# Moving the next group's norm, window sums and patch copies to other places among the sampling tiles of a fused four-layer convolution kernel

## Time and profile before

| | us |
|---|---|
| median of 3 runs | 2766.87 (2762.34 to 2772.3) |
| the profiled execution's own time | 2759.06 |
| its span, first to last instruction | 2757.2 |
| PE, DVE, ACT busy | 2132.4, 1811.6, 1524.7 |
| from one front's second convolution to the next one's | 327.8 |

### The profile page before, as it was taken

One profiled execution on the slowest core, in us unless ns is written; L12 is line 12 of the kernel. 1 busy time (PEld: TensorE's weight loads), 2 busy tenths in 40 slices (PEclk: granted clock), 3 DMA queues, 4 the chain that ended last, 5 costly groups with the idle time before them and its releaser, 6 DMA issues.

```text
span 2757.2 us, 51316 instructions
## 1 busy us (share of the span) xinstructions
PE 2132.4 (77%) x20658; PEld 1792.4 (65%) x20658; DVE 1811.6 (66%) x3534; ACT 1524.7 (55%) x1803; POOL 24.7 (1%) x35
## 2 busy tenths in 40 slices
PE   0274488787886978878788778878788798887999
PEld 0223465687666966578666776568766696667998
DVE  3365458667686666866677665866758665776776
ACT  0021356466564655556565465646656465656987
POOL 1000000000000000000000000000000000000000
PEclk9686699899998989989999889989899899998999
DMA  6643533273351842436333453327434182113331
GB/s 171 126 132 72 141 106 120 76 161 113 100 147 43 202 123 78 125 92 181 103 105 104 111 155 106 116 79 161 119 98 148 44 199 92 52 48 90 108 116 56
DMA packets 290577, 311.50 MB, mean 113 GB/s; under 512 B 238148, under 2 KB 249092, under 8 KB 286116
## 3 DMA queue, kind: packets, MB, share of 16 engines
q1 hardware_dynamic: 285828, 273.74, 36.5%
q0 software_dynamic: 3360, 30.27, 4.1%
q10 hardware_dynamic: 1152, 4.19, 0.5%
HBM read 251.65 MB, written 56.48 MB: 112 GB/s over the span
## 4 chain that ended last, share of the span: by engine, by line
PE 53%; DVE 19%; DVEq 8%; SPq 7%; ACT 5%; DMA 4%; issue 4%; ACTq 0%; POOL 0%; POOLq 0%
PE bank L1014 37%; PE bank L1096 5%; SPq L369 4%; DVE code L884 4%; DVEq L883 4%; PE bank L1001 3%; DVE samp L713 3%; PE bank L1115 2%; SPq L319 2%; DVE strip L708 2%; PE bank L1074 1%; DVEq L712 1%; ACT diag L581 1%; PE bank L1132 1%; PE bank L1156 1%
## 5 line engine op out<-in xcount | busy, mean ns | idle before, releaser
L1014 PE MATMUL bank<-picture,tent 128*128 128x160 f32 x9216 | 1420.5, 313 | 79.1 <-DVE strip L708 52.2
L1014 PEld LDWEIGHTS bank<-picture,tent 128*128 128x128 f32 x9216 | 1351.5, 201 | 109.5 <-issue 83.2
L708 DVE TENSOR_TENSOR strip<-bank,near 128x480 f32<-128x480 f32 x768 | 503.6, 656 | 586.2 <-PE bank L1014 585.3
L514 ACT ACTIVATE tent<-zs,row_at_sb 128x1152 f32<-128x1152 f32 x512 | 614.5, 1249 | 50.5 <-DMA zs<-z_rows 50.3
L517 ACT ACTIVATE tent<-tent 128x2304 f32<-128x2304 f32 x256 | 543.8, 2124 | 18.8 <-issue 1.7
L713 DVE TENSOR_REDUCE samp<-strip 128x96 f32<-128x480 f32 x768 | 501.5, 653 | 72.4 <-issue 2.7
L504 ACT COPY samp_t<-bank 96x384 f32<-96x384 f32 x256 | 120.6, 471 | 461.9 <-PE bank L1001 461.8
L1115 PE MATMUL bank<-cb,xs 128*128 128x512 f32 x512 | 267.3, 624 | 118.6 <-DVE code L884 86.4
L1115 PEld LDWEIGHTS bank<-cb,xs 128*128 128x128 f32 x512 | 83.3, 191 | 259.4 <-issue 173.7
L574 ACT COPY xs<-xn 32x128 f32<-32x128 f32 x256 | 75.0, 293 | 195.6 <-PE bank L1115 177.8
L1001 PE MATMUL bank<-ident_sb,samp 128*96 128x128 f32 x768 | 138.5, 292 | 53.3 <-ACT fin L500 47.4
(11 more groups left out here) (125 smaller groups left out, 1061.5 us busy)
## 6 DMA issues: line engine op xcount, KB each, us to landing
zs<-z_rows SPq DMA_DIRECT2D x256, 576.0 KB, 4.2
picked_weights<-arena SPq DMA_DIRECT2D x15, 1800.0 KB
arena<-picked_weights SPq DMA_DIRECT2D x24, 720.0 KB, 6.6
arena<-windows SPq DMA_DIRECT2D x288, 50.0 KB, 4.0
slice<-picked_weights SPq DMA_DIRECT2D x16, 720.0 KB, 6.1
windows<-arena SPq DMA_DIRECT2D x32, 312.5 KB, 5.0
slice<-windows SPq DMA_DIRECT2D x192, 50.0 KB, 2.9
y_patches<-yc SPq DMA_DIRECT2D x32, 160.0 KB, 4.4
```

Of the source, the lines that this page charges most:

```text
L514: act.activation(w[:, c], zs[:, N % SPREADS, :], ACT.Abs, bias=row_at[:, c:c + 1])
L708: dve.tensor_tensor(y, STRIPS[j % 3][:, 0:DENSE * XW * C].rearrange("p (d c x) -> p d c x", d=DENSE, c=C), w.broadcast_to([128, DENSE, C, ...
L1014: m = pe.matmul(STRIPS[j % 3][:, XW * C * e:XW * C * (e + 1)], tent[:, N % TENTS, c, DENSE * d + e], picture[:, b % 2, i, c], start=(c == ...
```

## The change

DVE's `features(k)` becomes two parts: `normalise(k)` (wait for the input, norm) behind the gate of slice 2, and `features(k)` (the sums) behind the gate of slice 3. ACT's `root(k, 0)` moves to the place of the norm. The five copies of `windows(k)` move from the routing of the second layer to behind tile 0, and `copy_features(k)` from the second layer's pooling to behind tile 2, ahead of the wait for `y_in`. SP's `features(k)` becomes `features_out(k)`, the store, behind the last of the `ROW_SLOTS` and ahead of the stores of `y`, and `features_in(k)`, the load, where both were; its `windows(k)` moves ahead of `POOL_SLOTS`.

More of the change, by code:

```diff
@@ L330, in tiles, with features_out, features_in @@
                         store(b, 0)
-            def features(k):
+            def features_out(k):
                 sp.wait_ge(wsum_ready, k + 1)
                 sp.dma_start(sum_dram.rearrange("i (c n) -> (i c) n", c=C), wsum[:]).then_inc(wsum_out, 16)
+            def features_in(k):
                 sp.wait_ge(wsum_out, 16 * (k + 1))
@@ L385, in front @@
                         load_slice(g, v + SLICES)
+                    if v == NV - 1 and k:
+                        features_out(k)
                 full = MOST * C // PATCHES
@@ L400, in front @@
                 if k:
-                    features(k)
+                    features_in(k)
                 at(Y_SLOTS)
-                at(POOL_SLOTS)
                 if k:
                     windows(k)
+                at(POOL_SLOTS)
                 at(MIX_SLOTS)
@@ L435, in front @@
                         spread_rows(N)
-            features(0)
+            features_out(0)
+            features_in(0)
             windows(0)
@@ L555, in front @@
                     at(ROW_SLOTS[v])
-                if k:
-                    root(k, 0)
+                    if v == 2 and k:
+                        root(k, 0)
                 at(Y_SLOTS)
@@ L730, in _, with normalise, features @@
             grid0 = xp0[:].rearrange("p (h w) -> p h w", w=G0)
-            def features(k):
+            def normalise(k):
                 dve.wait_ge(x_loaded[k % KEPT], 16 * (k // KEPT + 1))
                 norm(k, 0, x_of(k), grid0[:, 1:H + 1, 1:W + 1])
+            def features(k):
                 dve.drain()
@@ L817, in front @@
                     gate(v)
+                    if v == 2 and k:
+                        normalise(k)
+                    if v == 3 and k:
+                        features(k)
+                first, end = Y_SLOTS
+                at((first, first + 1))
                 if k:
-                    features(k)
-                at(Y_SLOTS)
+                    windows(k)
+                at((first + 1, end))
+                if k:
+                    copy_features(k)
                 dve.wait_ge(y_in, 16 * 2 * IMG * (g + 1))
@@ L832, in front @@
                 dve.tensor_reduce(sm1[:, 0, 0:1], grid1, AX.XY, ALU.add)
-                if k:
-                    copy_features(k)
                 dve.drain()
@@ L842, in front @@
                 dve.tensor_tensor(sm1[:, 1, :], P0[:, 0:E1], broute[:], ALU.add).then_inc(z_ready, 1)
-                if k:
-                    windows(k)
                 dve.wait_ge(ez_ready, g + 1)
@@ L967, in front @@
                 at(REST_SLOTS)
+            normalise(0)
             features(0)
```

## The result

The changed kernel takes 2721.78 us (median of 4 runs, 2720.78 to 2726.64), the kernel before 2765.52 us on the same chip (4 runs, 2762.34 to 2772.3): a ratio of 0.9842 with a 95% interval of 0.982 to 0.9864. The kernel is 1.6% faster. The forecast was 2724 us.

The account below looks back on a forecast made before the run. PE was taken as the bound (53% of the chain), interrupted by DVE's long pieces between tiles. Per front 9.0 us gained less 2.3 lost, net 6.7, six times is 40 us off: 2724 us, range 2706 to 2744.

Parts of the forecast that it names:

- 6.3 us for leaving the place behind the last slice, less 0.8 and 0.6: Slice 4 to pooling, per front: 6.3 us gained without norm and sums; sums' new place costs 0.8, copies' 0.6.
- 0.9 us at tile -3: Norm behind slice 2's gate makes DVE late for PE's turn behind the next tile's first strip: 0.9 us lost per front.
- ACT's root: nothing: ACT waiting for the moved norm's variance delays no tents, being back before 1600.18: no loss, bounds 0 and 2.4 us.
- 2.7 us for the copies: Pooling's product to second convolution: the five copies leaving DVE's block there gain 2.7 us per front, bounds 2.1 and 3.8.
- SP: nothing in the fronts with tiles: SP's sums store ahead of y starts y about 3 us late, still hidden: no loss, bounds 0 and 3.2 us.
- Front 0: nothing, within -2 and +3: Front without tiles: y up to 3.2 us later, copies give 2.3 back; taken as nothing, bounds -2 and +3 us.
- The clock: PE's matmuls behind waits run at half rate, so removing a wait returns more than its length: about 2 us per group.
- The sum: Fronts 1 to 6: 9.0 us gained less 2.3 lost, net 6.7 us each, 40 us in all; chance 62%.
- Nothing is lost in the new places: Rival: DVE's moved pieces cost PE nothing beside its waits for tents; 54 us off, 2711 us; chance 18%.
- Only the copies pay: Rival: norm and sums cost 6.3 us in their new places too; 13 us off in all, 2752 us; chance 10%.
- The slower case, no run-ahead: Rival: each moved piece stops PE for its whole length plus slow restart; 36 us slower, 2802 us; chance 4%.
- The chain takes it back: Rival: a later unmoved wait, for tents' rows or gathered weights, swallows the gain; 2762 to 2770 us; chance 6%.

Follow-up runs that it names:

- e1: The kernel before with only the five copies moved behind tile 0 and their store ahead of tile 3; 2756.34 us, ratio 0.9973.
- e2: The changed kernel with the five copies and their store back in the old place; norm and sums stay moved; 2735.24 us, ratio 0.9893.
- e5: The changed kernel with norm and sums together behind slice 2's gate; 2737.3 us, ratio 0.9896.
- e3: The changed kernel with norm and sums together behind slice 1's gate, ACT's root with them; 2720.09 us, ratio 0.985.
- e6: The changed kernel with the norm and ACT's root behind slice 0's gate and the sums behind slice 1's; 2717.97 us, ratio 0.9826.
- e4: The changed kernel with SP's store of the sums back behind the stores and loads of y; 2724.3 us, ratio 0.9849.
- e8: e6 with two copies behind tile 0, three behind tile 1, routing behind tile 3 and gates behind tile 5; 2705.1 us, ratio 0.979.
- e9: e8 with the norm cut: statistics, variance and ACT's root behind slice 0, scaling and sums behind slice 1; 2706.57 us, ratio 0.9785.

## Why the prediction was right

- **The bound.** PE is the bound and DVE's long pieces between tiles interrupt it. Shown by e1, e2 and e5: each piece costs where it stands, by what is left of it over what PE has to do.
- **6.3 us for leaving the place behind the last slice, less 0.8 and 0.6.** Slice 4 to the pooling fell by 4.7 us against 4.9 in the sum. The three terms apart: e2, without the copies there, 34.4 us, so the copies cost 0.6 us; e3, e5 and e6, without the sums there, 33.9 to 34.1, so the sums cost 0.9 to 1.1 us (0.8 forecast).
- **0.9 us at tile -3.** Right in size, for the most part by luck. From slice 3's convolution to slice 4's PE took 12.5, 12.9 and 12.5 us in fronts 2, 3 and 5 before, and 13.3, 13.7 and 13.3 us after, 0.8 us more in each, and the same in all three profiles (fronts 4 and 6 have other waits there). The cause given, DVE late with its samples at the second turn, shows only in front 3. There PE's timeline has 0.37 us for ACT's copy of a result and 0.49 us for DVE; fronts 2 and 5 have the 0.37 us alone:

```profile
935.62 0.50 PE L1012 MATMUL bank<-ident_sb,samp 128*96 128x128 f32 x3 [0.37 <-ACT fin L505]
941.51 0.53 PE L1012 MATMUL bank<-ident_sb,samp 128*96 128x128 f32 x3 [0.49 <-DVE samp L718]
```

  The step "ACT's root: nothing" failed by the first. I counted ACT free at 1598.34, but the copy of the result (L505), 0.25 us of ACT, stands behind the root in the new order, and the turn of tile -4 waits for it. ACT waits for the variance at 935.12 us here, 2.36 us long:

```profile
935.12 0.20 ACT L498 ACTIVATE sd<-ve 128x1 f32<-128x1 f32 x1 [2.36 <-DVE ve L659]
935.22 0.25 ACT L505 COPY fin<-bank 128x128 f32<-128x128 f32 x1
```

- **2.7 us for the copies.** The stretch fell by 2.6, 2.8 and 3.2 us in the three profiles, and by 3.2 in e1. The copies' own share is less certain than that: in e2, where they stay, the stretch is already 0.7 us shorter than before. The wait of 0.7 us for the exponential, which took the copies' place, is there with 0.66 us.
- **SP: nothing in the fronts with tiles.** Right: no wait for y or features at tile 2, and e4 changes nothing there. SP's stores of y in fact began at 1273.78 us, behind the sums at 1273.37, and the features' load at 1286.45, 6.6 us ahead of the end of tile 2.
- **Front 0: nothing, within -2 and +3.** Its second convolution came 2.0 us later in the first profile, 2.9 and 5.1 in the others, where part of it is already there in the slices. y was to come up to 3.2 us later; DVE's addition came 5.0 us later. The greater part is y itself. SP could store its first part only behind the sums (112.82 us against 108.49), and the last loads of y left 4.55 us later; first before, then after:

```profile
120.09 1.28 SPq L398 DMA_DIRECT2D arena<-y_patches  x4
```

```profile
124.64 1.28 SPq L402 DMA_DIRECT2D arena<-y_patches  x4
125.97 0.77 SPq L338 DMA_DIRECT2D feat<-window_means  x1
```

  Before, DVE began 4.5 us behind the first of these; with the same 4.5 us y would have been there at 129.2 (my estimate), and `copy_features` held DVE until 129.42. So the term that was mis-sized is the wait of y, 4.5 us and not 3.2; the wait for the features, which the prediction missed, adds only some 0.4 us to it. In e4 y's loads leave at 120.18 again, and there the features alone hold DVE, until 127.53: 1.9 us less than in the changed kernel.
- **Front 1: 6.7 us like the others.** From front 0's second convolution to its own it took 229.4 us before and 223.3, 226.1 and 222.3 in the three profiles: 6.1, 3.3 and 7.1 us less.
- **The clock.** The slow matmuls went (3.54 to 1.90 us, 2.78 to 1.87 us), and the granted clock was 0.50 over the twelve at 1298.06 and 1.00 over those at 1281.84 after. But the prediction took this for about 2 us a group of PE's path, and most of it wasn't on the path. Behind such a wait PE needs DVE's samples at the next turn, 3.27 us behind the start of the twelve, whether these took 2.78 us (before) or 1.87 us (after). At the first wait it was the same before the change: in front 3 the twelve took 2.82 us, and PE waited for DVE:

```profile
970.63 2.82 PE L1014 MATMUL bank<-picture,tent 128*128 128x160 f32 x12 [4.18 <-DVE strip L708]
973.90 0.87 PE L1001 MATMUL bank<-ident_sb,samp 128*96 128x128 f32 x3 [0.45 <-DVE samp L713]
```

  What the clock cost is what lies behind that turn: 4.07 us from 1349.32 to the convolution before, 3.63 us from 1329.10 after, 0.4 us. At the first wait turn to turn is 5.78 us before (1301.39 to 1307.17), 5.25 us for the same work where PE had not stopped (1284.03 to 1289.28), 0.5 us. So a wait taken away did bring back more than its length, but by about half a microsecond. The 6.3 us didn't suffer from it, since they were read as a whole from front 4 against front 7.
- **The sum.** 6.7 us per front were forecast; the profiles give 5.5, 6.2 and 7.2 (periods of 322.1, 321.4 and 320.4 against 327.6). The spread is in every stretch but that from slice 4 to the pooling. In the first profile the 32.4 us are made up of 27.8 in fronts 2 to 6, 6.1 in front 1 and 0.8 in front 7, less 2.0 lost in front 0 and 0.3 behind front 7's convolution. The forecast took 40 us off; the medians of the three measurements are 43.7, 40.5 and 37.2 us below those of the kernel before on the same chips. So the 40 us are right, and that 2724 lies within 2.3 us of the first median is in part luck.
- **The rivals.** "Nothing is lost in the new places" fell by the waits of 0.93 and 0.48 us, though it nearly holds for the places that e8 uses. "Only the copies pay" fell by e2. The slower case, no run-ahead, fell by every profile; e5 shows how a piece looks that PE can't cover, at about 4 us a front. "The chain takes it back": not for the gain behind slice 4, but exactly so for the 1.3 us of e9.

## What to carry to other kernels

When an engine that isn't the bound holds up the one that is, list its pieces between the tiles, and for each place work out the overhang: what it has to do up to the next thing the bound needs, less what the bound has to do meanwhile. A piece that needs a third engine doesn't fit in an idle time which that same engine causes; put there what needs nobody. Matmuls that run slowly behind a wait cost time only if PE, and not the engine it waits for next, sets the pace there. And before shaving the last microsecond, ask which wait stands next in the stream: if its releaser doesn't wait for you, it will grow by what you saved.

## What the runs showed of the hardware that I had not expected

The stretch from the second convolution to slice 0 has the same instructions in every front, and its length takes steps of about 2.5 us: 207 to 208, about 210, 212.5 in most cases; 207.6 us in front 4 of the changed kernel and 209.8 in front 5. The windows view, below, has a row for each: the window and its length, the busy time and count of PE, its weight loads, DVE, ACT and POOL, then the granted clock, 0.93 in the first and 0.91 in the second, the DMA share and GB/s. PE's busy time is 168.83 and 173.29 us. In the kernel before all five were 207.8 to 207.9 in its one profile.

```profile
1010.80:1218.40 207.60, 168.83 (x1364) 131.84 (x1367) 145.05 (x290) 117.23 (x157) 1.00 (x1) 0.93 0.33 92
1332.70:1542.50 209.80, 173.29 (x1361) 134.11 (x1363) 145.69 (x291) 117.43 (x157) 1.00 (x1) 0.91 0.31 90
```

Over the three profiles of the changed kernel the granted clock of this stretch is 0.93 in the fronts of 207 to 208 us and 0.90 in those of 212.5 us; those of about 210 us have 0.91 to 0.93. Two of these, front 2 of the first profile (209.9 us) and front 6 of the third (210.3), have 0.93 like the short ones, so the clock goes with the length in most cases and not in all. In this stage PE pauses often for DVE's search of the best code. That the steps come from products that meet the lower clock behind some of these pauses fits the rows, but is not shown, and what decides it was not tried. They move between profiles of one kernel. Over fronts 2 to 6 they add from 1 us (the changed kernel's third profile) to 15 us (e5) to the 1039 us of before, enough to hide or feign a gain, which is why the table by stretch and not the total was used to test the terms.
